# Edge features on 64 partitions per block: one transfer in 2 KB runs, a first-layer product of 64 rows, four feature products of 64 rows

## The reference, cut to what matters

```python
h = jnp.maximum(_layernorm(x, axis=-1), 0.0)
h0 = pe_val @ W0 + b0                 # 412500 x 32 @ 32 x 64
t = gelu(h0) @ W1 + b1
t = gelu(t) @ W2 + b2
score = (h0 + t) @ W3 + b3
msg = h[src] * score
sums = segment_sum(msg, dst, n)
wV = sums / maximum(cnt, 1.0)
out = x + wV @ Wo + bo
```

## Time and profile before

| | |
|---|---|
| median of three executions | 4045.06 us |
| span of the profiled execution | 4042.3 us |
| what the median has beyond that span | 2.8 us |
| PE busy | 3264.8 us (81%), mean granted clock 0.785 of 2.4 GHz |
| DVE busy | 1084.3 us (27%) |
| ACT busy | 585.2 us (14%) |
| POOL busy | 3045.3 us (75%) |
| DMA traffic | 174.70 MB, 43 GB/s in the mean |

### The profile page before, as it was taken

How to read it: one execution, slowest core, us unless ns; L and a number is a source line. 1 busy time by engine, 2 the same in 40 slices (tenths; PEclk the granted TensorE clock), 3 DMA queues, 4 the chain that set the end, 5 groups by cost and what they waited for, 6 DMA issues and landing times.

```text
span 4042.3 us, 34777 instructions
## 1 busy us (share of the span) xinstructions
PE 3264.8 (81%) x12308; PEld 2146.4 (53%) x12309; DVE 1084.3 (27%) x2563; ACT 585.2 (14%) x838; POOL 3045.3 (75%) x3228
## 2 busy tenths in 40 slices
PE   4988888888888878888888788888887788888879
PEld 2655555555555555555555555555555555555557
DVE  7322222222222222222222222222222222222234
ACT  4211111111111111111111111111111111111111
POOL 7777777777777777777777777777777777777776
PEclk8977777777777777777777777777777777777778
DMA  5211111111111111111111111111111111111112
GB/s 145 48 40 40 40 40 40 40 40 40 40 40 42 40 40 40 40 40 40 40 40 40 40 40 40 40 40 40 41 41 41 40 40 40 40 40 40 40 37 60
DMA packets 217372, 174.70 MB, mean 43 GB/s; under 512 B 112108, under 2 KB 163821, under 8 KB 216920
## 3 DMA queue, kind: packets, MB, share of 16 engines
q0 software_dynamic: 103136, 105.82, 12.1%
q1 hardware_dynamic: 113536, 64.91, 6.0%
q10 hardware_dynamic: 616, 3.20, 0.2%
HBM read 167.28 MB, written 6.40 MB: 43 GB/s over the span
## 4 chain that ended last, share of the span: by engine, by line
POOL 73%; issue 24%; PE 2%; DVE 0%; DMA 0%; POOLq 0%; ACT 0%; DVEq 0%
POOL rows L332 73%; PE ps_h1a L539 0%; PE ps_h1b L539 0%; PE ps_h0a L463 0%; POOLq L353 0%; PE ps_h1b L471 0%; PE ps_h1a L471 0%; PE ps_sb L482 0%; PE ps_sb L477 0%; PE ps_wa L497 0%; PE ps_h0b L463 0%; DMA rows<-h_rows,idx 0%; PE ps_sb L486 0%; PE ps_sa L482 0%; PE ps_sa L477 0%
## 5 line engine op out<-in xcount | busy, mean ns | idle before, releaser
L332 POOL DMA_INDIRECT rows<-h_rows,idx x3175 | 2999.5, 945 | 967.6 <-issue 966.9
L497 PE MATMUL ps_wa<-ln_sq,msg 128*128 128x128 f32 x1616 | 350.1, 385 | 665.6 <-DVE msg L690 665.5
L497 PEld LDWEIGHTS ps_wa<-ln_sq,msg 128*128 128x128 f32 x1616 | 299.2, 276 | 741.2 <-issue 728.1
L690 DVE TENSOR_TENSOR msg<-ps_sa,rows 128x512 f32<-128x512 f32 x202 | 139.7, 691 | 1403.3 <-DMA rows<-h_rows,idx 1391.0
L690 DVE TENSOR_TENSOR msg<-ps_sb,rows 128x512 f32<-128x512 f32 x201 | 139.0, 692 | 1396.8 <-DMA rows<-h_rows,idx 1382.0
L396 ACT ACTIVATE g<-ps_h1a,wp 128x512 f32<-128x512 f32 x202 | 139.0, 688 | 2383.5 <-PE ps_h1a L471 2383.5
L482 PE MATMUL ps_sa<-w_attr,attr 128*128 128x256 f32 x808 | 405.0, 654 | 0.0
L482 PEld LDWEIGHTS ps_sa<-w_attr,attr 128*128 128x128 f32 x808 | 229.8, 314 | 327.0 <-issue 292.6
L477 PE MATMUL ps_sa<-b_last,wp 1*128 1x512 f32 x404 | 403.1, 1097 | 0.0
L486 PEld LDWEIGHTS ps_sa<-w_gelu,g 128*128 128x128 f32 x1616 | 377.5, 321 | 34.3
L486 PE MATMUL ps_sa<-w_gelu,g 128*128 128x128 f32 x1616 | 367.7, 405 | 0.0
(11 more groups left out here) (94 smaller groups left out, 2381.4 us busy)
## 6 DMA issues: line engine op xcount, KB each, us to landing
attr<-in_edges SPq DMA_DIRECT2D x402, 128.0 KB, 3.0
rows<-h_rows,idx POOLq DMA_INDIRECT x3175, 2.4
xs<-in_x SPq DMA_DIRECT2D x4, 700.0 KB
h_rows<-ln_d ACTq DMA_DIRECT2D x4, 700.0 KB
dst_i<-in_dst SPq DMA_DIRECT2D x1, 1612.0 KB, 27.2
idx<-in_src SPq DMA_DIRECT2D x50, 32.0 KB, 2.3
rows<-in_dst_rows SPq DMA_DIRECT2D x4, 384.0 KB
out<-ln_d SPq DMA_DIRECT2D x1, 1530.0 KB
```

The source lines that it names most:

```text
L332: pool.indirect_dma_start(rows[:, slot, t, :], None, table, bass.IndirectOffsetOnAxis(ap=idx[:, part, at, t:t + 1], axis=0),).then_inc(gat ...
L497: pe.matmul(window[0:m * D, 0:m * WIN], msg[:, s % 2, t:t + m, :].rearrange("p t d -> p (t d)"), hot[:, k, t:t + m, :].rearrange("p t n -> ...
L690: dve.tensor_tensor(msg[:, s % 2, 0:n, :], ps_s[s % 2][:, 0:n * D].rearrange("p (t d) -> p t d", d=D), rows[:, s % G_RING, 0:n, :], ALU.mu ...
```

## The change

The two transfers of a pair of blocks become one. A block now lies on 64 partitions (group, feature), all 512 columns in one run of 2 KB; the even block of a pair is on partitions 0 to 63 and the odd one on 64 to 127. The semaphore target is 16 per pair in place of 32. The first layer is one product of 64 rows and 512 columns in place of two of 128 rows and 256 columns. The score's feature part is four products of 64 rows and 128 columns in place of two of 128 rows and 256 columns. The odd block uses the copies of the weights on partitions 64 to 127.

```diff
-        attr = sb("attr", [4 * DE, IN_RING, 2, P])
+        attr = sb("attr", [4 * DE, IN_RING // 2, HALF])
@@ load_attr
-                halves = edges[b:b + n, :, :, :].rearrange("o g f (j c) -> j (g f) o c", j=2)
-                for j in range(2):
-                    sp.dma_start(attr[j * 2 * DE:(j + 1) * 2 * DE, half * 2:half * 2 + n, :, :
-                                      ].rearrange("p o k e -> p o (k e)"), halves[j]
-                                 ).then_inc(attr_in[half], 16)
+                sp.dma_start(attr[0:n * 2 * DE, half, :],
+                             edges[b:b + n, :, :, :].rearrange("o g f c -> (o g f) c")
+                             ).then_inc(attr_in[half], 16)
@@ first
-                    pe.wait_ge(attr_in[s // 2 % (IN_RING // 2)], uses(b, IN_RING) * 32)
-                for j in range(2):
-                    mm = pe.matmul(ps_h0[s % 2][:, j * 2 * P:(j + 1) * 2 * P], w_in[:, j, :],
-                                   attr[:, s % IN_RING, :, :].rearrange("p k e -> p (k e)"),
-                                   start=(j == 0), stop=(j == 1), skip_group_check=True)
-                mm.then_inc(h0_done, 1)
+                    pe.wait_ge(attr_in[s // 2 % (IN_RING // 2)], uses(b, IN_RING) * 16)
+                o = s % 2
+                pe.matmul(ps_h0[s % 2][:, :], w_in[o * 2 * DE:(o + 1) * 2 * DE, o, :],
+                          attr[o * 2 * DE:(o + 1) * 2 * DE, s // 2 % (IN_RING // 2), :], start=True, stop=True
+                          ).then_inc(h0_done, 1)
@@ last
-                for k in range(2):
-                    four = ps_s[s % 2][:, :].rearrange("p (j k c) -> p k j c", j=2, k=2)[:, k, :, :]
-                    pe.matmul(four, attr[:, s % IN_RING, k, :],
-                              w_attr[:, :].rearrange("p (j c) -> p j c", j=2), start=False, stop=False, skip_group_check=True)
+                o = s % 2
+                for j in range(TILES // 2):
+                    pe.matmul(ps_s[s % 2][:, j * 2 * D:(j + 1) * 2 * D],
+                              attr[o * 2 * DE:(o + 1) * 2 * DE, s // 2 % (IN_RING // 2), j * P:(j + 1) * P],
+                              w_attr[o * 2 * DE:(o + 1) * 2 * DE, o * 2 * D:(o + 1) * 2 * D],
+                              start=False, stop=False, skip_group_check=True)
```

## The result

| executions, us | before | changed |
|---|---|---|
| median | 4045.01 (7) | 4059.49 (7) |
| lowest to highest | 4044.60 to 4045.24 | 4053.24 to 4059.73 |

The ratio is 1.003, 95% interval 1.0021 to 1.004: slower by more than the 0.2% that can be told apart. The forecast was 4049.8 with a range up to 4054.0. The changed kernel's executions lie in two groups, three at 4053.2 to 4053.9, inside that range, and four at 4059.5 to 4059.7, outside it and with the median among them; the kernel before has one group. The profiled execution, 4053.33, is of the lower group: span 4051.5, 9.2 us above the 4042.3 before.

The account below looks back on a forecast made before the run. POOL's gathers were taken to bound the kernel, with PE catching up only at the end. 24 new switches (22 x 0.19 + 2 x 0.38 = 4.94 us) less 0.15 to spare added 4.8 to 4045.06: 4049.8 us, range 4044.6 to 4054.

Parts of the forecast that it names:

- POOL is the bound, and the long stretch hides the change: Long stretch: POOL needs 9.99 us a block, PE idles 2.1, so 0.57 to 1.14 us more PE work is hidden.
- The transfer costs nothing: Loads of block pairs: one issue fewer and half the packets cost nothing, bounds -0.1 to +0.1 us.
- A switch costs 0.19 us: PE's end stretch: each row-count change costs a 0.09 gap and 0.10 exposed load; 24 new ones, 4.94 us.
- The first two switches fall into the half-clock part: Start of PE's catch-up at the end: two of 24 new switches doubled to 0.38 us each, the other 22 at 0.19.
- the range's upper end: Whole time: 4054 us, from switches a third dearer (+1.6), columns (+0.5) and some of the exposed loads.
- The clock falls: Rival, all of PE: 1.2 GHz all along, a block 11.9 us against POOL's 9.99, about 4860 us; chance 0.03.
- 0.15 us to spare: Block 402's last message: PE finishes 0.15 us before the sums start, taken off the 4.94 us of switches.
- Weight loads exposed at 64 rows: Rival, feature products and first layer: loads wait for products, 7.7 us on top of 4.8, 4057.6 us; chance 0.13.

Follow-up runs that it names:

- rows128: The changed kernel's transfer and layout, but first layer and feature products on all 128 rows with zero weights: 4052.81 us, kernel before 4052.56 on that chip.
- rows128_2: rows128 run again on another chip: 4045.19 us, kernel before 4045.16 there.
- last64: rows128 with only the feature products on 64 rows, first layer kept at 128: 4054.61 us, kernel before 4052.56 on that chip.
- first64: rows128 with only the first layer on 64 rows, feature products kept at 128: 4059.16 us, kernel before 4052.56 on that chip.
- gaps2: rows128 plus a product of one zero row and 16 columns after the first layer: 4048.80 us, kernel before 4044.55 on that chip.
- bias128: The changed kernel with its bias product on 128 rows in place of one: 4051.40 us, kernel before 4044.55 on that chip.
- dense: The changed kernel plus three 128-row, 512-column products where PE waits for DVE before second(394): 4049.70 us, kernel before 4044.55 on that chip.
- before2: The kernel before, unaltered, as a run of its own: 4045.07 us, against 4045.16 for the kernel before beside it.
- after8: The changed kernel, unaltered, run again on one of two chips where it takes 4781.4 to 4790.9 us.

## Why the prediction was wrong

- *POOL is the bound, and the long stretch hides the change*: right. 945 ns a gather, the last at 4029.48, PE idle 1.2 us a block (1 to 1.5 forecast).
- *The transfer costs nothing*: right, by rows128 and rows128_2, within their intervals.
- *A switch costs 0.19 us, at 64 rows as at one, three more a block, 24 in the end stretch*: right. Block 6.54 us (6.5 forecast), the first layer at the bias's 1.05, block 402's message released by PE; last64's ten switches cost 2.1 us (1.9 and 0.3 for the columns, less 0.15), alone. The Trainium skill (TensorEngine Tiling (Array Packing), Tiling Modes) has the drain at a change of mode; with 64 rows the trace now agrees in that each change costs, 0.19 us, though it shows a gap and an exposed load and not what makes them. At half clock I had doubled it; the bias there takes 2.00 us against 1.71 for the plain columns, so 0.3 is nearer than 0.38.
- *The first two switches fall into the half-clock part*: this is the step that failed, and with it the sum had no term for a later clock. It took over from the earlier trace rows that the clock is at 1.00 within 4 us of second(394), and by first64, gaps2 and bias128 it is so because 128-row products follow one another there for three steps. With 64 rows in `first` between them, and the one-row bias behind, it rises 13 to 15 us after second(394), or a block later still. That makes 4.3 us in the lower group (dense takes them away), which with the 4.9 and the later start is the 9.2 measured between the two profiles. The median, 4059.49, is of the upper group, some 6 us more; two blocks at half clock have that size, but its cause stays open. That the lower group lies inside the range is in part luck: the range's upper end was made of dearer switches and exposed loads, none of which came.
- *The clock falls* was a rival, with 4860 us and a chance of 0.03, and set aside because the one-row bias runs at 1.00 without pulling it down. That was the wrong question: the clock, once up in the end stretch, stayed up to the last sums in every profile but those with PE's unexplained gaps; what few rows change there is when it comes up. In the long stretch they lower the share of time at full clock (0.75 against 0.78 in the mean), which costs nothing under POOL's pace. The price lay between the rival's and none, and no case of mine had it. The trace of the kernel before had a warning too: ahead of 3973 PE works without a gap at 65-row products and stays at 0.50 (the window is in the last section).
- *0.15 us to spare*: as a number of one execution right, as a property wrong. The end moves with the clock's rise, 3.6 or 5.5 us, by 1 us, and the profiled execution was one with an early rise. The prediction set that one profile's slack against a median 1.0 us above it, and before2, with a time near the median, had none left.
- *Weight loads exposed at 64 rows*: did not happen; eight loads and products take 1.08 us, that is 0.89 and one switch.

## What to carry to other kernels

A product with fewer rows was no cheaper here: it streams the same columns (0.86 us for two passes of 512), and each change of the row count costs a gap and an exposed weight load, 0.19 us. Where a layout wants two operands stacked on one partition range, multiplying all 128 rows with zero weights for the part not meant cost nothing that could be told (rows128). And where a stage is bound by an engine that has just been at half clock, ask not only what its instructions cost but what they do to the moment of the rise; a few dense products while it waits can be worth more than they take (here 2.0 us taken, 6.15 given back). That was tried on the changed kernel alone, and it stayed 5.2 us behind the kernel before.

## What the runs showed of the hardware that was not expected

- PE without a gap is not PE at full clock. 37 us of 65-row projections stand at 0.50 in both kernels (they differ from the other products in columns too, so this alone does not single out the rows), and so do 12.9 us (26.2 in after8) of a block with 64-row and one-row products among 128-row ones. The Trainium skill (TensorE: Matmul & The Clock Gate, Why this matters for your kernels) advises to keep TensorE busy and free of idle gaps for full throughput; here that did not suffice, and exchanging one row for 128 in a single product (bias128) brought the rise 5.5 to 7.7 us forward. The window of the projections, of the kernel before:

```profile
3934.00:3971.00 37.00, 37.00 (x170) 37.00 (x170) 19.68 (x51) 0.00 (x0) 28.16 (x30) 0.50 0.12 26
```

- POOL's gathers have a pace that is not the kernel's: 1.249 us in most profiles, 1.251 in the four on one chip, where the last gather begins at 4037.1 to 4037.4 in place of 4029.2 to 4029.9: almost 8 us, more than most effects here. It is not the chip's alone: the kernel before has one execution of 4044.17 there, and the profiles of gaps2 and bias128 show a pace in between on a chip where the others have 1.249.
- On two chips both kernels took 4781 to 4792 us, for a reason that the profiles do not name; one of the two, by its number, is the one on which the kernel before had taken 4052.56 earlier.
